# A two-layer conv/scan/attention kernel: skip term on VectorE, MLP ended in row 93, gating products on GpSimd

## The reference, cut to what matters

```
# layer 0, per sample and direction (forward, and backward on flipped tokens)
u = silu(conv1d(u) + b);  delta = softplus(dt @ W + b)
h = exp(delta * A[n]) * h + delta * u * Bm[n]         # 16 states n
y = sum_n h * Cm[n] + u * D_param                      # u * D is the skip term
y = y * silu(z)                                        # the gating product
out = y @ out_proj_w                                   # both directions are summed
...
x = x + res_scale * (scale_mod * (fwd + bwd) + sigmoid(conv3x3(xn)) * xn)
# layer 1
t = t + attention(layernorm(t)) @ Wo + bo
t = t + gelu(layernorm(t) @ w_fc.T) @ w_proj.T
```

## Time and profile before

| | before |
|---|---|
| median of 3 runs | 4229.28 us (4217.98 to 4236.39) |
| the profiled execution | 4223.39 us |
| span of its trace | 4221.6 us |
| busy: PE, DVE | 80%, 85% |
| busy: ACT, POOL | 61%, 65% |
| mean granted TensorE clock | 0.877 |

### The profile page before, as it was taken

One profiled execution on the slowest core, in us unless ns is written; L12 is line 12 of the kernel. 1 busy time (PEld: TensorE's weight loads), 2 busy tenths in 40 slices (PEclk: granted clock), 3 DMA queues, 4 the chain that ended last, 5 costly groups with the idle time before them and its releaser, 6 DMA issues.

```text
span 4221.6 us, 40649 instructions
## 1 busy us (share of the span) xinstructions
PE 3382.0 (80%) x11610; PEld 1701.1 (40%) x11626; DVE 3587.6 (85%) x2721; ACT 2560.3 (61%) x3547; POOL 2733.4 (65%) x1692
## 2 busy tenths in 40 slices
PE   6503398978898798978889788988989789976997
PEld 2201145623364234732356233742356233641472
DVE  4999898998899998998989988999989998898121
ACT  3533557766675656756676666757667576765362
POOL 2888676676766767676766767667766777676000
PEclk9756699988999899988999899988999889997998
DMA  3999798887978889787978879888988889788000
GB/s 81 232 229 239 189 225 185 208 201 191 216 187 204 208 196 211 182 208 181 238 180 220 190 193 221 189 196 193 222 190 195 202 200 219 178 208 207 6 7 15
DMA packets 224024, 785.11 MB, mean 186 GB/s; under 512 B 25292, under 2 KB 40958, under 8 KB 223518
## 3 DMA queue, kind: packets, MB, share of 16 engines
q0 software_dynamic: 117504, 427.87, 52.4%
q1 hardware_dynamic: 106270, 354.32, 25.6%
HBM read 339.60 MB, written 39.85 MB: 90 GB/s over the span
## 4 chain that ended last, share of the span: by engine, by line
PE 35%; DVE 25%; issue 13%; DMA 11%; POOL 8%; ACT 7%; DVEq 0%; SPq 0%; ACTq 0%; POOLq 0%
DVE pB L1198 17%; PE pW L668 9%; PE pW L585 9%; DMA y<-hb 7%; POOL hb L1375 6%; PE pW L473 4%; DMA y<-area 3%; PE pW L516 3%; PE pW L601 2%; ACT pt L1002 2%; PE pW L735 2%; DVE hb L1207 2%; PE pW L550 2%; POOL y L1386 1%; DVE pB L1163 1%
## 5 line engine op out<-in xcount | busy, mean ns | idle before, releaser
L1198 DVE TENSOR_TENSOR_SCAN pB<-pB,hb 128x1024 f32<-128x1024 f32 x768 | 1757.0, 2288 | 40.2 <-POOL hb L1375 20.1
L1386 POOL DMA_DIRECT2D y<-hb x768 | 747.3, 973 | 736.6 <-DVE hb L1207 627.6
L1375 POOL TENSOR_TENSOR hb<-du_f,b_row 128x1024 f32<-128x1024 f32 x384 | 1036.8, 2710 | 131.9 <-DMA b_row<-bc_rows 108.3
L1375 POOL TENSOR_TENSOR hb<-uc_b,b_row 128x1024 f32<-128x1024 f32 x384 | 995.3, 2593 | 61.8 <-DMA y<-hb 60.2
L1207 DVE TENSOR_TENSOR hb<-pB,c_row 128x1024 f32<-128x1024 f32 x768 | 940.4, 1224 | 44.3
L821 ACT ACTIVATE pB<-delta,vec 128x1024 f32<-128x1024 f32 x384 | 428.8, 1117 | 383.7 <-DVE hb L1207 383.3
L821 ACT ACTIVATE pB<-xres,vec 128x1024 f32<-128x1024 f32 x384 | 429.1, 1119 | 325.7 <-DVE hb L1207 325.0
L668 PE MATMUL pW<-area,pt 128*128 128x64 f32 x3456 | 432.6, 279 | 20.0 <-ACT pt L1002 12.4
L668 PEld LDWEIGHTS pW<-area,pt 128*128 128x128 f32 x3456 | 405.0, 193 | 69.8 <-ACT pt L1002 59.7
L1242 DVE TENSOR_REDUCE stat<-pW 128x1 f32<-128x640 f32 (+7 forms) x361 | 258.7, 753 | 163.4 <-PE pW L588 163.4
L492 PE MATMUL pW<-area,xn_area 128*128 128x512 f32 x576 | 265.4, 616 | 41.5 <-DVE area L1285 27.0
(11 more groups left out here) (172 smaller groups left out, 4890.7 us busy)
## 6 DMA issues: line engine op xcount, KB each, us to landing
y<-hb POOLq DMA_DIRECT2D x768, 512.0 KB, 7.2
b_row<-bc_rows SPq DMA_DIRECT2D x256, 512.0 KB, 5.8
c_row<-bc_rows SPq DMA_DIRECT2D x256, 512.0 KB, 5.5
du_f<-in_x SPq DMA_DIRECT2D x8, 1536.0 KB, 13.6
kept_residual<-in_x SPq DMA_DIRECT2D x8, 1536.0 KB, 13.0
y<-area POOLq DMA_DIRECT2D x24, 512.0 KB, 8.0
xres<-kept_residual SPq DMA_DIRECT2D x8, 1536.0 KB, 10.5
out_x<-xa SPq DMA_DIRECT2D x8, 1536.0 KB, 6.8
```

The lines of the kernel that those rows point to most:

```text
L1198: dve.tensor_tensor_scan(flow(d, buf), flow(d, buf), flow(d, hb[r % NHB][:, :]), 0.0, ALU.mult, ALU.add).then_inc(scan_done, 1)
L1375: pool.tensor_tensor(hb[r % NHB][:, :], du[d][:, k, :], b_row[g % 2][:, :], ALU.mult)\
L1386: pool.dma_start(y[:, k, :], hb[r % NHB][:, :], accum_op=ALU.add).then_inc(y_in[k], 16)
```

## The change

The backward skip term moves: in one row of each group (`SKIP` = rows 21, 19, 20 for k = 0, 1, 2) DVE writes its product by `c_row` back into the bank and then adds u * D with a scalar_tensor_tensor. ACT's product, its buffer and POOL's three DMAs go. The gating products of the sample in front move to POOL, behind its tap adds; for the last sample DVE keeps them. POOL's three residual DMAs (L1400) move behind the inputs of rows 0 to 2. `S1` is 61 for 62, the steps behind it are closer, so that the MLP ends in row 93 for 95. Projections `wo` run in the order of token halves and start after fewer copies; the three adds of a half share a row. ACT copies the B and C rows ahead of the step size. DVE's samples are written out, with no loop.

```diff
-SKIP = (24, 27, 30)
+SKIP = (21, 19, 20)
-          + [(kind, k, (22, 26, 29)[k] + i) for k in range(KT)
+          + [(kind, k, (22, 25, 28)[k] + i) for k in range(KT)
-S0, S1 = 33, 62
+S0, S1 = 33, 61
...
-    + [("wo_add", t, S1 + 3 + t // 2) for t in range(6)]
+    + [("wo_add", t, S1 + 2 + t // 3) for t in range(6)]
...
-    + norm(1, S1 + 5, S1 + 7, S1 + 8, S1 + 10, S1 + 11)
+    + norm(1, S1 + 4, S1 + 6, S1 + 7, S1 + 9, S1 + 10)
...
-    + [("mlp_in", 0, S1 + 12), ("mlp_cast", 0, S1 + 13), ("mlp_split", 0, S1 + 14)] + mlp(0, S1 + 14) + mlp(1, S1 + 24), key=lambda x: x[2])
+    + [("mlp_in", 0, S1 + 11), ("mlp_cast", 0, S1 + 12), ("mlp_split", 0, S1 + 13)] + mlp(0, S1 + 13) + mlp(1, S1 + 23), key=lambda x: x[2])
...
                 elif kind == "wo":
-                    pe.wait_ge(ct_evac, at(6, a, 6))
-                    if n >= 4:
+                    if n < 4:
+                        pe.wait_ge(ct_evac, at(6, a, n + 3))
+                    else:
                         pe.wait_ge(wo_add, at(6, a, n - 3))
...
+                if r == SKIP[k]:
+                    dve.tensor_tensor(pBC[r % 2][:, :], pBC[r % 2][:, :], c_row[g % 2][:, :], ALU.mult)\
+                       .then_inc(skip_step, 1)
+                    dve.wait_ge(uc1_ready, at(3, b, 3))
+                    dve.wait_ge(skip_step, at(KT, b, sorted(SKIP).index(r) + 1))
+                    dve.scalar_tensor_tensor(out=hb[r % NHB][:, :], in0=uc[1][:, k, :], scalar=vec[:, k, V_D:V_D + 1],
+                                             in1=pBC[r % 2][:, :], op0=ALU.mult, op1=ALU.add).then_inc(m2_done, 1)
...
-            samples(dve, iteration)
+            for b in range(NB + 1):
+                iteration(b, b < NB, b > 0, b < NB - 1)
...
+            def gated(b):
+
+                for k in range(KT):
+                    pool.wait_ge(y_in[k], at(YIN, b, YIN))
+                    pool.wait_ge(zs_ready, at(3, b, k + 1))
+                    pool.tensor_tensor(zs[:, k, :], y[:, k, :], zs[:, k, :], ALU.mult).then_inc(yz_ready, 1)
...
                         input_row(b, r)
+                        if r < KT:
+                            keep_local(b, (1, 0, 2)[r])
                         if r >= LAG:
                             sum_row(b, r - LAG)
-                        if r in SKIP:
-                            sum_skip(b, SKIP.index(r))
```

86 lines of the change are left out of this document (36 added, 50 removed).

## The result

The changed kernel took 4321.8 us in the median of four runs (4314.9 to 4323.9) beside 4225.9 us for the kernel before in the same session (four runs, 4218.0 to 4236.4): a ratio of 1.0223, 95% interval 1.0196 to 1.0249. It is slower: the interval lies wholly above 1. The profiled execution has a span of 4318.7 us (before 4221.6), so 97.1 us are to be found.

The account below looks back on a forecast made before the run. DVE, busy 85% of the span, was taken as the bound. Terms 6 + 28.5 + 12.6 + 40 - 2 = +85 us on 4223.4 give 4308, some 4314 as shown median; forecast 4310, 8-in-10 range 4238 to 4340.

Parts of the forecast that it names:

- the forecast mechanism: Late accumulations at the boundaries plus waits in the projections make the kernel slower, 4310 us; chance 0.58.
- The boundary: Between samples: bulk transfers start early and delay the last accumulations, silu_u at T + 14.5, scan at T + 52.5; +40 us.
- Branch and gating products: At the boundary: taking both off DVE does not move the end, since DVE waits for the softplus behind them anyway.
- The output projection: Rows 63 and 64: three adds together wait for PE, delivering 2.86 us apart, while the norm's wait goes; +28.5 us.
- The decay of row 71: Copies for next_in stand ahead of this decay, so DVE waits 2.1 us in six samples; +12.6 us.
- The skip term: Backward rows: 4.05 us more DVE work per sample, mostly given back by shorter waits; +6 us.
- The tail: Behind sample 7: the projection starts some 2 us earlier; -2 us.
- Boundary pays, rows do not: Rival: accumulations land early, silu_u at T + 5.8, boundaries -5 us, whole +40 us, 4269; chance 0.17.
- DVE's own work decides: Rival: all work and waits removed from DVE at boundaries count, projection adds without waits; 4171 to 4186; chance 0.08.
- worse than forecast: Rival: PE idles between convolution and steps_in, its clock falls, silu_u at T + 17; 4345; chance 0.06.
- Nothing moves: Rival: boundaries give some 25 us, halfway between two other rivals; skip, projection and decay cost half; 4228; chance 0.11.
- `local` beside the products on GpSimd: Boundary: the third local could stand up to 2.4 us behind a gating product, in time when DVE waits for ACT.

Follow-up runs that it names:

- Experiment 1: Changed kernel with the three bulk transfers held until the sample's accumulations into y have landed: 4265.4 us.
- kernel of 7: Kernel before with only the changed rows of output projection, norms and MLP; skip term and gating products stay in their old places: 4317.3 us.
- experiment 4: Changed kernel with the gating products back on VectorE, behind local: 4323.4 us.
- experiment 9: Kernel before with changed output projection, norm and MLP rows, residual's two transfers held, next sample's projection ahead of second norm, output projection's additions two to a row: 4230.9 us.
- Experiment 3: Changed kernel with the next sample's projection ahead of the second norm: 4301.6 us.
- Experiment 8: Kernel before with the skip term alone on VectorE: 4235.1 us; then also with the moved projections and step sizes and the exchanged copies: 4255.4 us.
- 6: Changed kernel with bulk transfers held, next sample's projection ahead of the second norm, and output projection's additions two to a row: 4217.7 us.
- experiment 2: Changed kernel with parts of the bulk transfers held: only out_x free, 4266.9 us; out_x and xres free, copy into the kept residual held, 4304.9 us.

## Why the prediction was right, and where its terms were off

The forecast was 4310 us, by late accumulations at the boundaries and waits in the projections; it came to 4321.8, and the forecast mechanism decided. That the total is only 12 us off is partly luck: the terms were 22 us too small in four places and 10 us too large in two. By its steps:

**The boundary (+40; measured +47)** held as reasoned. Every boundary's silu waits for `y<-hb`, 10 to 17 us where I asked for 10 or more, and starts at T + 12.6 to T + 14.7 (I took 14.5). Experiment 1 takes the cause away and 56 us with it. The scan comes at T + 53 where I had 52.5. The 38 us behind the silu, taken from sample 0 of the kernel before, became 38.4 to 39.4: I had priced the exchange of the two copies at 0.8 us behind sample 0 alone, and it counts at every boundary. With it TensorE's eight products of the first step sizes take 5.1 to 6.6 us at a granted clock of 0.55 to 0.71. The kernel without the exchange (7) has boundaries shorter by 10 us in sum, more than the 7 that this term lacks; it also differs in the skip term, the gating products and the jump, so the share of the exchange is argued, not shown.

**Branch and gating products (0)**: right, for the gating products shown by experiment 4, for the branch argued from the same wait. The cover is VectorE's 9.6 us of waiting, and experiment 9 shows what the branch costs when it is gone. Of the three gating products on GpSimd, the first and the third take 2.36 us as the tap additions do, and the second 3.3; the mean of 2.68 mixes them (see below).

**The output projection (+28.5; measured +24.1)**: right in kind, its waits of 1.82, 0.28 and 1.82 us sit where I put 2.2, 0.75 and 2.1, and the 1.0 us before the second addition is not there. The size was off because I took TensorE's mean of 2.86 us a projection from before. There only the first was slow, 4.1 us, with a granted clock of 0.91 over the six, and the others came 2.58 us apart; in the changed kernel all do, at 1.00.

**The decay of row 71 (+12.6; measured 3.9 us a sample, six times)**: the mechanism was right, the size was not: 23.4 us of waits where I had 12.6. The replay had 2.1 us a sample; the second copy waits for TensorE until 2378.2 in sample 4, and the scan behind its decay has then lost 3.9. Experiment 3 gives 25 us of rows back. Against it stand 8 us that I had not seen: in five samples the MLP's first addition no longer waits for TensorE (1.3 to 2.1 us each).

**The skip term (+6; measured about 0 in the changed kernel, +10.6 alone)**: in the changed kernel VectorE's added work came as I had it (27.0 us over samples 1 to 7, I took 28.4), and the waits before the backward step sizes gave back 14.7 us, 2.1 a sample where I had 2.3. By place it was otherwise: in sample 4 the first of the three waits is 1.61 us, near the 1.9 that I gave, and the third grew from 2.59 to 3.39. My reason, that "the copies of the projections are no longer late", does not stand by itself: with the skip term alone the copy waits longer (4.46 us instead of 2.69) and only 4.7 us come back. Experiment 8 was to show that the moved rows make the difference, and did not. Rows 19 to 33 are as slow with the skip term on ScalarE in the kernel of 7 (481.0 us) as in the changed kernel (482.4); there VectorE waits 72.9 us for the step sizes instead of 51.4, so most of the added work lies inside that wait. In the kernels with the cures (6 against 9) rows 0 to 33 differ by 3.8 us. Why the term costs 10 us alone stays open.

**The tail (-2; measured +6.7)**: failed. I had the boundary's mechanism and did not apply it behind the last sample. There too `out_x` and `xres` start before the last accumulations, and VectorE's last gating products wait for them:

```profile
3990.32 1.23 DVE L1172 TENSOR_TENSOR zs<-y,zs 128x1024 f32<-128x1024 f32 x1 [5.52 <-DMA y<-hb]
```

With the transfers held the tail is 331.0 us instead of 335.1; the other 2.6 us of this term were not followed.

**The rivals.** "Boundary pays, rows do not" needed a silu at T + 5.8; that is what the hold gives (T + 5.0), so its reasoning on the boundary was sound and its condition was not met. "DVE's own work decides" fell: VectorE's share of the span went down. The clock part of "worse than forecast" came true: at boundaries 1 to 6 TensorE pauses 3.2 to 4.5 us before `steps_in` where it paused 0.8, and the granted clock over its twelve products is 0.64 to 0.79 where it was 1.00. But the silu never came at T + 17, and behind it the boundary took 38.4 to 39.4 us. "Nothing moves" holds a slip: halfway between -5 and -62 lies -34, not -25, so its time would be 4219; no chance or bound hangs on it.

On the DMA: the accumulations stand on GpSimd's queue, the bulk transfers on SyncE's. With all held the silu starts at T + 5.0, with the residual's read in flight some 5 us later, with the memory-to-memory copy as well some 9. The Trainium skill (DMA: Bandwidth & Descriptors, Queues, rings and completion order) has each engine take the waiting queues in turn, a packet at a time. The packets of experiment 2 agree where both queues move (68 to 67, 70 to 70), and a turn counts for more when the other queue's packets are of 39 KB. That the accumulation's first packet leaves 5.5 us after its issue instead of 1.4 does not follow from that rule, and stays open. Half of the engines would also not have meant a silu near T + 6, as the prediction has it: twice the 4.5 us from issue to landing is T + 9.3, about what experiment 2 measured with the copy held.

On `local` beside the products on GpSimd: the third `local` (`prob`, both inputs in SBUF) takes 1.30 us (1.28 before), since it starts ahead. It is GpSimd that waits: the second gating product, which starts 0.2 us behind that `local`, takes 3.3 us at all seven boundaries and the other two 2.36.

```profile
L1366 POOL TENSOR_TENSOR zs<-y,zs x21: 2332/2369/3332, 502.2 to 3524.4; 128x1024 f32<-128x1024 f32 x21
```

The Trainium skill (SBUF — State Buffer, Who interferes with whom) lets whichever of the two issues first go through and blocks the other. This case agrees, from both sides: the second gating product here, and in experiment 8 VectorE's product of 3.44 us beside a GpSimd input of 2.36 that started with it. The prediction had looked at the wrong one of the two; it costs nothing here, where GpSimd waits for the step sizes behind it anyway.

## What to carry to other kernels

When a step that others wait for is moved earlier, follow what its end sets free: here a vector addition ended 11 us earlier, counted from T, and with it 4.7 MB of transfers nobody needed yet ran into the small ones that everybody waited for. Holding the transfers back gave 66 us at the boundaries and the tail, cost some 9 in the rows behind, and was worth 56 us in all. An operation taken off the busiest engine gains nothing while that engine waits for another right behind it, and may gain once that wait is cured: try such an edit again after each cure.

## What the runs showed of the hardware

- A 512 KB accumulating transfer took 4.5 us from issue to landing with the bulk transfers held, and 13.5 us beside three transfers of 1536 KB on another queue, the first of which was nearly done.
- Two queues with packets of 4 KB moved one for one (68 to 67). The memory-to-memory copy moved in packets of up to 48 KB, and beside them the other queue fell from 33 packets in a microsecond to 8.
- In two places an operation of VectorE and one of GpSimd that each had both inputs in SBUF did not overlap: whichever began later took about as much longer as the other still ran, 1.0 us for GpSimd's and 2.2 us for VectorE's.
- TensorE's short products in the boundary ran at full granted clock behind short pauses, and mostly below it behind longer ones; not always, since with all transfers held, behind sample 5, the twelve ran at 1.00 (5.36 us) behind a pause of 3.8. Before, sample 4, at 1.00:

```profile
2456.33 5.36 PE L528 MATMUL pW<-area,xp_w 128*56 128x512 f32 x12 [0.78 <-ACT area L832]
...
2462.96 3.69 PE L564 MATMUL pB<-narrow,mixed 25*128 25x512 f32 x8 [1.27 <-ACT narrow L793]
```

  In the changed kernel, at 0.78 and 0.55:

```profile
2510.17 6.84 PE L528 MATMUL pW<-area,xp_w 128*56 128x512 f32 x12 [3.17 <-ACT area L833]
2519.34 6.54 PE L564 MATMUL pB<-narrow,mixed 25*128 25x512 f32 x8 [2.33 <-ACT narrow L795]
```

- The small store of B and C, 128 KB, landed within 2.0 us in the changed kernel (issued 2518.08, the next issue behind it on its queue 2520.07), where the residual's accumulations stand in rows 0 to 2; in the skip term's kernel of experiment 8, where they stand ahead of it, it took 6.4 us (2471.67 to 2478.04). That they are the cause was not tried apart.
